# A bound for 16 heads from weight norms instead of measured maxima, in a two-layer recurrent block on one core

## What is computed

```python
xn = _layernorm(x)
s = attention with one head of 128 (Wq, Wk, Wa, Wv, Wb), softmax over 1024 keys
g = silu(ternary MLP 128 -> 512 -> 512 -> 512 -> 128)
x = x + s * g
xn = _layernorm(x)
# second layer, s: 8 heads of 64, q and k give a softmax over heads, a decaying scan over the rows, Wo, a norm
s = _L1_attn_ref(xn, ...)
# second layer, g: 16 heads of 8, softmax over 1024 keys, plus a mixture of 8 experts (two of them used)
qkv = (x @ W_qkv + b_qkv).reshape(B, S, 3, 16, 8)
attn = softmax(einsum('bqhd,bkhd->bhqk', q, k) / sqrt(8)); attn_out = einsum('bhqk,bkhd->bqhd', attn, v)
g = silu(attn_out + moe_out)
x = x + s * g
```

## Time and profile before

| | us |
|---|---|
| median of 3 runs | 1051.15 |
| lowest, highest | 1050.69, 1057.59 |
| the profiled execution | 1052.17 |
| its span | 1050.3 |
| PE busy in the span | 980.8 (93%) |
| ACT busy | 759.2 (72%) |
| DVE busy | 560.3 (53%) |
| POOL busy | 197.7 (19%) |

### The profile page before, as it was taken

The page is one execution under the profiler, slowest core; times in us unless marked ns, Lnnn a source line. Parts: engine busy times, 40 slices in busy tenths (PEclk is TensorE's granted clock), DMA queues, the critical chain, the costliest instruction groups (busy, mean ns, idle before and its releaser), DMA issues.

```text
span 1050.3 us, 16258 instructions
## 1 busy us (share of the span) xinstructions
PE 980.8 (93%) x6122; PEld 548.5 (52%) x6122; DVE 560.3 (53%) x1372; ACT 759.2 (72%) x926; POOL 197.7 (19%) x144
## 2 busy tenths in 40 slices
PE   3999899999999989999989989999999998999995
PEld 2788633343478843334358874334436886333431
DVE  6655734635546653554564574455446457346252
ACT  5444699989753479998955358998885436999885
POOL 1100202512300020341130002043122002025023
PEclk9999899999999999999999999999999999999998
DMA  6000032000000013100000002300000000310000
GB/s 239 1 2 1 13 49 50 1 2 1 5 19 2 1 30 49 34 1 2 1 21 2 1 1 46 65 3 1 1 1 21 2 1 13 50 30 1 1 1 23
DMA packets 14428, 20.66 MB, mean 20 GB/s; under 512 B 2848, under 2 KB 11136, under 8 KB 14080
## 3 DMA queue, kind: packets, MB, share of 16 engines
q1 hardware_dynamic: 14336, 19.41, 8.6%
HBM read 7.85 MB, written 2.10 MB: 9 GB/s over the span
## 4 chain that ended last, share of the span: by engine, by line
PE 76%; DVE 8%; ACT 7%; issue 6%; POOL 2%; DMA 0%; DVEq 0%; POOLq 0%; ACTq 0%
PE ps L1097 73%; ACT big L1053 4%; PE ps L1501 1%; DVE st L277 1%; DVE wk L543 1%; POOL st L867 1%; DVE xn L449 1%; DVE wk L733 1%; ACT xn L1025 1%; ACT qz L1001 1%; DVE wk L474 1%; DVE flags L417 1%; PE ps L1117 1%; DVE qk_max L558 0%; PE ps L1494 0%
## 5 line engine op out<-in xcount | busy, mean ns | idle before, releaser
L1053 ACT ACTIVATE big<-ps 128x1024 f32<-128x1024 f32 x512 | 493.8, 1034 | 50.8 <-PE ps L1097 48.7
L1097 PE MATMUL ps<-big,vaug 128*32 128x512 f32 x2048 | 272.6, 604 | 3.8 <-DVE wk L733 2.6
L1097 PE MATMUL ps<-hid 32*128 32x512 f32 x1024 | 130.6, 493 | 3.7 <-ACT big L1053 2.5
L1097 PE MATMUL ps<-hid,fw_sb 128*128 128x512 f32 x416 | 100.7, 396 | 0.0
L969 ACT ACTIVATE wk<-ps,cols_sb 128x512 f32<-128x512 f32 x64 | 40.5, 687 | 78.3 <-PE ps L1097 74.3
L867 POOL TENSOR_TENSOR st<-st 128x4 f32<-128x4 f32 x16 | 16.2, 1011 | 423.3 <-DVE st L532 315.2
L1097 PEld LDWEIGHTS ps<-hid 32*128 32x128 f32 x1024 | 49.1, 181 | 77.2 <-issue 41.6
L1097 PEld LDWEIGHTS ps<-hid,fw_sb 128*128 128x128 f32 x416 | 77.7, 188 | 17.8
L880 POOL TENSOR_TENSOR qz<-qz,wk 128x512 f32<-128x512 f32 x32 | 41.1, 1286 | 232.8 <-DVE wk L703 232.8
L1097 PEld LDWEIGHTS ps<-big,vaug 128*32 128x32 f32 x2048 | 41.0, 108 | 69.8 <-issue 42.2
L721 DVE SCALAR_TENSOR_TENSOR big<-ps,sm,big 128x128 f32<-128x128 f32 x128 | 44.2, 345 | 46.9 <-PE ps L1097 35.9
(11 more groups left out here) (210 smaller groups left out, 1618.5 us busy)
## 6 DMA issues: line engine op xcount, KB each, us to landing
hid<-spl SPq DMA_DIRECT2D x288, 32.0 KB
xnext<-in_x SPq DMA_DIRECT2D x4, 512.0 KB, 3.9
out<-qz SPq DMA_DIRECT2D x8, 256.0 KB, 2.3
big<-in_fw SPq DMA_DIRECT2D x1, 1877.0 KB, 8.9
wk<-in_lw SPq DMA_DIRECT2D x1, 1476.0 KB, 13.9
big<-in_fw SPq DMA_DIRECT2D x1, 939.0 KB, 10.7
cst_sb<-in_cst SPq DMA_DIRECT2D x1, 440.0 KB, 4.4
xn<-in_aw SPq DMA_DIRECT2D x1, 320.0 KB, 5.0
```

Of the source, the lines that this page charges most:

```text
L1053: up(ms_exp, a.activation(prob[:, at:at + 2 * CH].rearrange("p (h n) -> p h n", n=CH), ps[:, bank:bank + 2, :], ACT.Exp, scale=HDM ** -0.5))
L1097: return t_.matmul(out_, lhsT, rhs, start=start, stop=stop, **kw)
```

## The change

- The bound is made once, in setup and batch 0, from the norms of the weights' columns: DVE squares 256 columns of `lw_hi` between the first and second row maximum, PE sums them over rows, DVE scales by 128, POOL takes the square root, and DVE adds absolute biases and multiplies, in front of batch 0's first gated unit. The product with `ones` and `bias_q` follow in batch 0's turn, on DVE ahead of `mq_rest(0)` and the residual, with the read of the flag that chooses the branch. In batches 1 to 3 all of that is gone, as are the four maxima in every batch, and a product of one column and a read of the flag on PE.
- DVE's order in the turn: `mq_rest(0)` stands ahead of `residual(1)`, `mq_rest(1)` ahead of `block_normalise(1)`, `split_rest` between `product(0)` and `product(1)`.
- PE's order: `stack(0)` and `values_unit(0)` ahead of the transposes, `stack(1)` behind them, `mq_units(1)` (now in banks 0 and 1 again by its own index, waiting for the first two stacks' copies), `qk_unit(2)`, `stack(2)`, `stack(3)`, `qk_unit(3)`, `qk_unit(4)`. Scores start in bank 0 instead of 2.
- ACT: the three fills of k's frames are gone; `stacked(0)` and `(1)` stand around `split_head`, `(2)` and `(3)` ahead of the table load. In the tiles with a `qk` side piece `q_unit` stands between the two exponentials.
- SP: four DMAs write ones into rows 24 to 31 of k's frames (from `one_row`, 128 floats repeated), when the MLP's last products are done. The 72 copies go by group: all 24 of group 1, then of 2, then of 3.
- POOL fills q's frames when the normalised rows are there, since `bias_q` exists by then.

```diff
-S_BANKS, S_FIRST = 6, 2
+S_BANKS, S_FIRST = 6, 0
-QK_BANKS = ((2, 3), (4, 5), (2, 3), (4, 5), (0, 1), (6, 7), (6, 7))
-MQ_BANKS = (0, 1)
-STK_BANKS = (6, 7, 6, 6)
+QK_BANKS = ((2, 3), (4, 5), (2, 3), (6, 7), (4, 5), (6, 7), (6, 7))
+MQ_BANKS = (0, 1, 0, 1)
+STK_BANKS = (0, 1, 0, 1)
+BOUND_BANK, VALUES_BANKS = 6, (7, 7, 7)
...
+        squares = qz[:, 2, 0:2 * D]
...
@@ SP
-                for j, which, first in ((1, 0, True), (1, 1, False), (0, 0, True), (0, 1, False)):
...
+                sp.wait_ge(w3_mm.sem, w3_mm.at(b, 2))
+                for g in range(GH):
+                    rows_ = slice(QUAD * g + 3 * HDM, QUAD * (g + 1))
+                    up(ones_in, sp.dma_start(k_st[rows_, 1:NG, :].rearrange("p g (a n) -> p (g a) n", n=P).bitcast(F32),
+                                             one_row[0:HDM, :].bitcast(F32).unsqueeze(1).broadcast_to([HDM, (NG - 1) * S // P, P])), 16)
+                sp.wait_ge(qfill_ok.sem, qfill_ok.at(b, NG - 1))
+                sp.wait_ge(mq_hi.sem, mq_hi.at(b, 4))
+                for g4 in range(1, NG):
+                    for j, which in ((1, 0), (0, 0), (1, 1), (0, 1)):
...
+                        if g4 == 1 and (j, which) == (1, 1):
+                            sp.wait_ge(mq_lo.sem, mq_lo.at(b, 4))
@@ DVE, start of a batch
                 for t in range(NT):
                     row_maximum(t)
+                    if b == 0 and t == 0:
+                        v.wait_ge(lw_hi_ok, 1)
+                        w_ = lw_hi[:, LM:LM + 2 * D].bitcast(F32)
+                        done(v.tensor_tensor(squares, w_, w_, ALU.mult), "squares")
+                    if b == 0 and t == 2:
+                        v.wait_ge(setup_p, 5)
+                        done(v.tensor_scalar(norms, ps[:, 1, 0:2], float(D), 1e-30, ALU.mult, ALU.max), "norms")
+                        biases = cols_sb[:, COL["mbq"]:COL["mbq"] + 2]
+                        done(v.scalar_tensor_tensor(qk_max[:, 2:4], biases, -1.0, biases, ALU.mult, ALU.max))
...
                 if b == 0:
+                    v.wait_ge(norm_ok, 1)
...
+                    done(v.tensor_tensor(qk_max[:, 4:6], norms, qk_max[:, 4:6], ALU.mult))
...
+                    done(v.tensor_tensor(qk_max[:, 4:6], qk_max[:, 4:6], qk_max[:, 2:4], ALU.add))
...
+                    done(v.scalar_tensor_tensor(qk_max[:, 6:7], qk_max[:, 4:5], -1.002, qk_max[:, 5:6], ALU.mult, ALU.mult))
...
+                    done(v.tensor_scalar(sm[:, 7, 0:HM], cst_sb[:, CBM:CBM + HM], qk_max[:, 6:7], None, ALU.mult), "bound rows")
@@ DVE, turn
                 split_rest(xt_lo, xt_hi, T_BANKS[0], 0, xT_mm, 1, x_hi, x_lo)
+                if b == 0:
+                    v.wait_ge(bnd_mm, 1)
+                    limit = ps[:, BOUND_BANK, 0:HM]
...
+                    need_max = v.value_load(iflag[0:1, 1:2], min_val=0, max_val=1)
+                mq_rest(0)
                 residual(1)
                 block_stats(1)
-                mq_rest(0)
+                mq_rest(1)
                 block_normalise(1)
-                mq_rest(1)
                 product(0, QK_BANKS[0][1])
+                split_rest(xt_lo, xt_hi, T_BANKS[1], 1, xT_mm, 2, x_hi, x_lo)
                 product(1, QK_BANKS[1][1])
-                mq_maximum(0)
-                mq_maximum(1)
-                split_rest(xt_lo, xt_hi, T_BANKS[1], 1, xT_mm, 2, x_hi, x_lo)
                 values_in(0)
-                mq_maximum(2)
-                mq_maximum(3)
...
                 mq_rest(2)
+                mq_rest(3)
                 product(2, QK_BANKS[2][1])
...
                 product(3, QK_BANKS[3][1])
                 product(4, QK_BANKS[4][1])
@@ POOL
+            g_.wait_ge(setup_v, marks["norms"])
+            g_.tensor_tensor(qk_max[:, 4:6], qk_max[:, 0:2], half[:, 0:2], ALU.pow).then_inc(norm_ok, 1)
...
                 for g4 in range(1, NG):
-                    g_.wait_ge(bnd_ok.sem, bnd_ok.at(b, 1))
+                    g_.wait_ge(bnd_ok, 1)
+                    g_.wait_ge(ln_ok.sem, ln_ok.at(b, 2))
@@ ACT, turn and tiles
-                for g4 in range(1, NG):
-                    a.wait_ge(w3_mm.sem, w3_mm.at(b, 2))
-                    up(kfill_ok, a.activation(k_st[:, g4, :], col("row24").broadcast_to([P, S]), ACT.Copy))
+                stacked(0)
                 split_head(xt_hi, T_BANKS[1], 1, xT_mm, 2, x_hi)
+                stacked(1)
                 mq_head(2)
                 mq_head(3)
                 q_unit(2, QK_BANKS[2][0])
-                stacked(0)
+                stacked(2)
+                stacked(3)
                 a.activation(mrow2[:, 0:1], ones[:, 0:1], ACT.Exp)
                 q_unit(3, QK_BANKS[3][0])
-                stacked(1)
-                stacked(2)
                 q_unit(4, QK_BANKS[4][0])
-                stacked(3)
...
                     for e_ in range(2 * k_, 2 * k_ + 2) if k_ < QUADS else ():
+                        if e_ % 2 and what == "qk":
+                            q_unit(i, QK_BANKS[i][0])
@@ PE
+                        t_.wait_ge(setup_v, marks["squares"])
+                        mm(ps[:, 1, 0:1], squares[:, 0:D], ones[:, 0:1], True, True)
+                        mm(ps[:, 1, 1:2], squares[:, D:2 * D], ones[:, 0:1], True, True).then_inc(setup_p, 1)
...
                 g_transposes(1)
+                if b == 0:
+                    t_.wait_ge(setup_v, marks["bound rows"])
+                    mm(ps[:, BOUND_BANK, 0:HM], ones, sm[:, 7, 0:HM], True, True).then_inc(bnd_mm, 1)
                 t_.wait_ge(pv_norm.sem, pv_norm.at(b, NT))
                 qk_unit(0)
                 qk_unit(1)
+                stack(0)
+                t_.wait_ge(res_ok.sem, res_ok.at(b, 2))
+                values_unit(0)
                 t_.wait_ge(ln_ok.sem, ln_ok.at(b, 2))
                 transposes(xnv, T_BANKS[1], 1)
-                values_unit(0)
-                t_.wait_ge(mq_lo.sem, mq_lo.at(b, 2))
+                stack(1)
+                t_.wait_ge(stk_ok.sem, stk_ok.at(b, 2))
                 mq_units(1)
                 t_.wait_ge(prod_ok.sem, prod_ok.at(b, 1))
                 qk_unit(2)
-                stack(0)
...
+                stack(2)
+                stack(3)
                 t_.wait_ge(mv_ok.sem, mv_ok.at(b, 1))
-                up(bnd_mm, mm(ps[:, SIDE_BANK, 0:HM], ones, sm[:, 7, 0:HM], True, True))
+                qk_unit(3)
                 t_.wait_ge(prod_ok.sem, prod_ok.at(b, 2))
-                qk_unit(3)
...
                 qk_unit(4)
```

More of the change, by code:

```diff
@@ L608, in _ @@
                 mq_rest(2)
+                mq_rest(3)
                 product(2, QK_BANKS[2][1])
-                v.wait_ge(bnd_mm.sem, bnd_mm.at(b, 1))
-                bound = ps[:, SIDE_BANK, 0:HM]
-                step(v.tensor_reduce(flags[:, 1:2], bound, AX.X, ALU.min))
-                own()
-                step(v.tensor_scalar(flags[:, 2:3], flags[:, 1:2], -SAFE * HDM ** 0.5, None, ALU.is_ge))
-                step(v.tensor_scalar(iflag[:, 1:2], flags[:, 1:2], -SAFE * HDM ** 0.5, None, ALU.is_lt))
@@ L617, in _ @@
-                own()
-                step(v.scalar_tensor_tensor(bias_w[:, :].rearrange("p (a g) -> p a g", g=GH),
-                                            bound.rearrange("p (a g) -> p a g", g=GH), flags[:, 2:3], in_quad, ALU.mult, ALU.mult))
-                own()
-                up(bnd_ok, v.tensor_reduce(bias_q[:, :], bias_w[:, :].rearrange("p (a g) -> p a g", g=GH), AX.X, ALU.add))
-                mq_rest(3)
                 product(3, QK_BANKS[3][1])
                 product(4, QK_BANKS[4][1])
-                need_max = v.value_load(iflag[0:1, 1:2], min_val=0, max_val=1)
```

92 lines of the change are left out of this document (39 added, 53 removed).

## The result

The changed kernel takes 1060.16 us (median of 20 runs, 1056.63 to 1064.43); the kernel before, on the same chips, 1053.92 (20 runs, 1049.86 to 1060.80). The ratio is 1.0053, 95% interval 1.0038 to 1.0068: about 5.6 us slower, inside the 1% that I called "same", but on the other side of it and outside the range of 1040.3 to 1049.0. The forecast started from a median of 1051.15, of three runs; the kernel before has 2.8 more over twenty, so that part of the distance from 1044.7 is no fault of a term. The profiled execution took 1058.19 us, span 1056.4, against 1052.17 and 1050.3: 6.0 more, where I forecast 6.4 less. 12.4 us are to be accounted for.

What follows compares the result with a forecast made beforehand. TensorE bounds the kernel (76% of the span). Batches 1 to 3 gain 6.9 us, transfers 1.6, batch 0 loses 2.05: 6.4 off the median of 1051.15 gives 1044.7 us, 8-in-10 range 1040.3 to 1049.0.

Steps and rivals of the forecast that it cites:

- the last one of the sum: TensorE's clock around the turn's transposes, left outside the sum: falls as often as before, same cost, 1.2 us a fall.
- rival C: Clock falls cost up to 2 us in all four batches (two idle pieces close together): 1049.7 us; chance 0.13.
- T to first scores: Each batch, second-half transposes to first scores of the 16 heads: 10.8 us in place of 13.03, gain 2.2.
- First to third scores: Each batch, first scores to third tile's: q's copy behind the first exponential starts earlier, gain 0.9 us.
- Ahead of T: Batches 1 to 3: a correction put in front of the residual makes the second-half transposes 0.8 us later.
- Transfers: 72 row copies sorted by head group end PE's waits, 1.6 us gained over the run; four constant transfers cost nothing.
- rival D: Constant-row transfers all use one DMA engine, second group's rows come late: 11 us a batch, 1089 us; chance 0.04.
- Squares: Setup, batch 0: DVE's squares blocked by POOL's subtraction, maxima end 1.9 us later; 0.6 if not blocked.
- Rows of the bound: Batch 0: four small dependent operations ahead of the first gated unit, on the chain, cost 0.85 us.
- The bound ahead of the residual: Batch 0's turn: product, chain, register read (0.3) and correction before the residual cost 2.4 us instead of 0.8.
- Rival B: The clock holds, or the squares aren't blocked: 10.1 us off the median, 1041.0 us; chance 0.18.

Runs made afterwards that it cites:

- e4: Changed kernel plus seven useless TensorE products ahead of the second half's transposes in batches 1 to 3; 1048.59 us, ratio to before 0.9956.
- e7: e6 with the seven extra products of e4 in all four batches; 1040.34 us, ratio to before 0.9856.
- e3: Kernel before with only q's copy for the sixth pair of products moved between the two exponentials; 1057.11 us, ratio 1.0025.
- e12: e11 with corrections behind the second half's residual and statistics, and values' products plus five extra ahead of the first stacked copy; 1040.28 us, ratio to before 0.9851.
- e10: Kernel before with eleven extra products ahead of the transposes in all batches and e3's moved q copy; 1049.68 us, ratio 0.9988.
- e11: e7 with e8's extra setup products and the norm products one score unit later; 1037.30 us, ratio to before 0.9843.
- e8: Changed kernel plus eighteen useless TensorE products in setup ahead of the wait for the flags; 1062.42 us, ratio to before 1.0081.
- e5: Changed kernel plus seven products in a never-taken branch of batch 1, so that later code lies further on; 1057.26 us, ratio to before 1.0014.
- e6: Changed kernel with squares, norm products, bound, flags and flag read moved behind batch 0's four gated units; 1053.39 us, ratio to before 0.9986.
- e2: Changed kernel with VectorE's read of the branch flag in batch 0 moved to just ahead of the branch; 1060.51 us, ratio to before 1.0053.

## Why the prediction was wrong

The step that failed is the last one of the sum: "I take it that the clock falls as often and costs the same." I had read the falls as something outside the change and gave the dearer clock 0.13. The runs show that the change made them: T to S lost to the clock, against the fed kernels (13.31 in batch 0 and 13.03 in the others for the old order, 10.32 for the new), 0.9 + 0.3 + 0.9 + 0 = 2.1 us before and 2.85 + 2.6 + 2.35 + 1.45 = 9.25 after. The forecast had 1.2 for a fall in batch 0, since it compared that batch with batch 3. Over the timed runs the shortfall, (1 - mean clock) times the span, went from 16.0 us (34 runs of the kernel before) to 23.7. I had moved nine products ahead of T, where PE idled, and so taken them from behind T, where they had stood ahead of the chunk's products: idle time in one piece became two pieces with thin work between. That the idle ahead of T is needed for the falls, e4 and e7 show; that it takes both pieces, or the nine products, is my reading, and no run moves those products alone. I had named the two pieces as a reason for rival C and put too little on it. C's mechanism was right and its price of 5 us for the four turns not far from the 7.1 found, but it alone would have given 1049.7.

The other terms:

- *T to first scores, 10.8 forecast.* 11.77 in batch 3. With the clock held 10.32, so the steps were right but for 0.5 us on the safe side, and that is the last one: in e4's batch 3 DVE's last product starts at T+10.06 (forecast T+10.0), and the scores follow in 0.27 in place of 0.8. The waits behind T came where I had put them (T+2.08 for T+2.0).
- *First to third scores, 0.9.* 0.83. Right. In the kernel before, half of it is taken back by waits for the copied rows (e3).
- *Ahead of T, 0.8 lost.* 0.70 by the trace, 0.6 by e12. Right.
- *Transfers.* The four new ones cost nothing that the waits show, and rival D didn't come. Against the kernel before at most 0.5 of the 1.6 us is to be seen between the turns. The fitter comparison is e10, which has the earlier scores but not the sorting: in e11 the four stretches behind S3 are together 1.55 us shorter than there, and the waits of 3.3 us are gone. No run sorts the copies alone.
- *Squares, 1.9 taken, 0.6 to 1.9 as bounds.* The block was right (3.89 and 0.42). By the rule of the Trainium skill ("SBUF — State Buffer", "Who interferes with whom") a DVE instruction with two SBUF inputs contends with a GpSimd one that reads SBUF, and whichever comes second is blocked for the whole instruction; the trace agrees. The pair of normalises that the prediction took as agreeing (0.94 against 0.60) is no case of it: it has one input in SBUF, and POOL's memset beside it only writes. The price was 2.75 at the end of the maxima. It had a part that I left out, PE waiting for the result (1.24 us, up to 1.87 in e8), with a clock fall behind it.
- *Rows of the bound, 0.85.* 1.4. With the squares the setup costs 3.8 us in the profile against 2.75, and 4 to 9 in four profiles.
- *The bound ahead of the residual, 2.4.* The register read was mis-sized: 2.2 us where I had 0.3. The read stood at the end of a list before, and from that place I priced it in the middle of one. Even there I had it too cheap: the first scores came 0.97 after the start of DVE's last product, and come 0.27 after it without the read (e4).
- *A stop of PE behind a branch, 4.1 us.* No term of mine. It goes with where the code lies (e5), so any edit may bring or remove it.

Set against the forecast, from the table: 4.1 for the stop, 3.6 for the turns of batches 1 to 3, 2.7 for batch 0's turn, 1.1 for the setup, 1.1 between: 12.6, for the 12.4 us to be accounted for.

Rival B (clock holds or squares aren't blocked) is what e7 brings about by hand. That its 1041.0 stands beside 1040.34 is partly luck: B is 10.1 us below a kernel before of 1051.15, e7 is 13.7 below one of 1054.06.

## What to carry to other kernels

Where the granted clock falls at a place in some executions before, a change that thins out TensorE's work there has its clock as the first term and not as a remark: price both levels, and try a few useless products in the idle stretch, which costs one loop. They kept the clock up in e4 and e7 and didn't in the setup (e8), so measure. Put one-time work where the engine idles longest, not where it is first possible: the same instructions cost about 7 us on the path (e6) and none to be seen behind the gated units. And look in the waits for "issue" in places that the change doesn't touch, before explaining a few us by the change: shift the code once and see whether they stay.

## What the runs showed of the hardware

- A read of a flag into a register stops VectorE's list for 2.20 us in its middle, though the flag had been written 0.5 us before the list came there; moved to the end of the list, the idle in the middle was gone, and PE waited 0.9 longer at the end (e2).
- A 128x256 multiply takes 0.42 us alone and 3.89 beside a GpSimd subtraction of 5.63.
- TensorE stopped for 0.68 to 2.68 us a few products behind a branch, in one batch of ten of the fourteen profiles; seven products in a branch that is never taken moved that stop to another batch (e5).
- With the clock nearly always at its upper level (mean 0.992 to 0.997), the six runs each of e7 and e11 lie within 2.1 and 1.7 us; those of the kernel before, at means of 0.973 to 0.992, within 11.
- Eighteen useless products in a gap of 5.24 us in the setup left the clock falling three times behind it (e8); seven in a gap of 1.65 us ahead of the transposes kept it at 1.00 (e4).
